# Issuing each 128-row gather as two gathers of 64 rows in a recurrent kernel's POOL stream

## The reference

```python
def step(h, inp):
    dAt, dBt, xt, Ct = inp
    h = dAt * h + dBt * xt[..., None]
    h_norm = jnp.sqrt(jnp.sum(h * h, axis=(1, 2), keepdims=True))
    scale = jnp.minimum(20.0 / (h_norm + 1e-08), 1.0)
    h = h * scale
    y = jnp.einsum('bdn,bn->bd', h, Ct) + Dp * xt
    return (h, y)
```

## Time and profile before

| | |
|---|---|
| device time, median of 3 runs | 1827.41 us (1826.48 to 1827.98) |
| the profiled execution's own time | 1828.65 us |
| its span, first to last instruction | 1826.9 us |
| busy: DVE | 1657.4 us, 91% |
| busy: PE | 1396.5 us, 76% |
| busy: ACT | 1082.4 us, 59% |
| busy: POOL | 932.5 us, 51% |
| L567, the power on POOL | 605.3 us in 1025 instructions |
| L539, gathers in the loop | 93.8 us in 80 instructions |
| L545, scatters | 91.9 us in 80 instructions |

### The profile page before, as it was taken

How to read it: one execution, slowest core, us unless ns; L and a number is a source line. 1 busy time by engine, 2 the same in 40 slices (tenths; PEclk the granted TensorE clock), 3 DMA queues, 4 the chain that set the end, 5 groups by cost and what they waited for, 6 DMA issues and landing times.

```text
span 1826.9 us, 38640 instructions
## 1 busy us (share of the span) xinstructions
PE 1396.5 (76%) x8889; PEld 1271.0 (70%) x8889; DVE 1657.4 (91%) x11513; ACT 1082.4 (59%) x2502; POOL 932.5 (51%) x1403
## 2 busy tenths in 40 slices
PE   6788979597968787697868786888859795879820
PEld 4577878496858687686758685877758685768720
DVE  7587999999998999999999999899999999899967
ACT  5775666556556654666565656566465655566424
POOL 5365555455555555455545554554555555555534
PEclk9858989898989899898989898898989898999965
DMA  9443011101020102100020102000110102010076
GB/s 334 149 202 95 20 32 45 51 19 35 19 76 23 30 19 65 31 23 29 21 74 24 30 24 71 22 25 27 41 51 22 35 19 74 21 31 22 18 247 223
DMA packets 97034, 110.47 MB, mean 60 GB/s; under 512 B 25680, under 2 KB 84176, under 8 KB 95632
## 3 DMA queue, kind: packets, MB, share of 16 engines
q1 hardware_dynamic: 87504, 86.26, 14.5%
q0 software_dynamic: 7776, 21.24, 3.7%
q10 hardware_dynamic: 1504, 0.22, 0.1%
HBM read 62.22 MB, written 45.48 MB: 59 GB/s over the span
## 4 chain that ended last, share of the span: by engine, by line
issue 38%; POOL 30%; DVE 22%; PE 6%; DMA 2%; POOLq 1%; ACT 1%; SPq 0%; DVEq 0%; ACTq 0%
POOL arena L567 22%; DVE arena L819 4%; DVE arena L790 3%; POOL moe L545 3%; POOL xrow L539 3%; DVE arena L804 3%; DVE arena L796 3%; DVE arena L811 3%; PE ps L1056 2%; DVE arena L815 1%; DVE arena L836 1%; DVE arena L793 1%; POOL arena L573 1%; DVE arena L808 1%; PE ps L1095 1%
## 5 line engine op out<-in xcount | busy, mean ns | idle before, releaser
L567 POOL TENSOR_TENSOR arena<-arena,neghalf 128x1 f32<-128x1 f32 x1025 | 605.3, 591 | 728.8 <-DVE arena L793 722.9
L815 DVE SCALAR_TENSOR_TENSOR arena<-arena 128x128 f32<-128x128 f32 x1024 | 360.5, 352 | 69.3 <-POOL arena L567 69.3
L1164 PE MATMUL ps<-ident,arena 128*128 128x128 f32 x1024 | 199.4, 319 | 228.8 <-ACT arena L908 190.1
L1164 PEld LDWEIGHTS ps<-ident,arena 128*128 128x128 f32 x1024 | 177.6, 245 | 252.7 <-issue 250.4
L983 ACT ACTIVATE arena<-ps,arena 128x128 f32<-128x128 f32 x1024 | 292.7, 373 | 53.7 <-PE ps L1168 52.8
L790 DVE TENSOR_TENSOR arena<-arena 128x128 f32<-128x128 f32 x1024 | 295.1, 288 | 23.6 <-issue 18.8
L1180 PE MATMUL ps<-arena,wf 128*128 128x256 f32 x1280 | 305.9, 387 | 10.9 <-ACT arena L995 10.9
L796 DVE CUSTOM_DVE_ANT_0 arena<-arena 128x128 f32<-128x128 f32 x1024 | 306.9, 300 | 0.0
L1168 PE MATMUL ps<-arena,pick 128*128 128x128 f32 x2048 | 286.6, 285 | 15.6 <-ACT arena L983 14.3
L804 DVE CUSTOM_DVE_ANT_0 arena<-arena 128x128 f32<-128x128 f32 x1024 | 292.6, 286 | 1.8 <-PE ps L1145 1.8
L1194 PE MATMUL ps<-wp,arena 128*128 128x256 f32 x1280 | 289.5, 379 | 0.0
(11 more groups left out here) (155 smaller groups left out, 1517.8 us busy)
## 6 DMA issues: line engine op xcount, KB each, us to landing
feed<-arena SPq DMA_DIRECT2D x9, 1024.0 KB, 3.9
arena<-feed SPq DMA_DIRECT2D x34, 256.0 KB
arena<-in_x SPq DMA_DIRECT2D x16, 512.0 KB, 6.4
moe<-zeros SPq DMA_DIRECT2D x8, 1024.0 KB, 9.5
wf<-in_c_fc SPq DMA_DIRECT2D x8, 1024.0 KB, 5.0
wp<-in_c_proj SPq DMA_DIRECT2D x8, 1024.0 KB, 6.0
arena<-moe SPq DMA_DIRECT2D x12, 512.0 KB, 8.6
arena<-dx SPq DMA_DIRECT2D x66, 64.0 KB
```

What stands on the lines that cost most here:

```text
L567: g.tensor_tensor(sv[:, slot, 1:2], mx, neghalf[:, 0:1], ALU.pow).then_inc(s_ready, 1)
L815: v.scalar_tensor_tensor(hr[:, slot, :], vv, sv[:, before, 1:2], ur[:, slot, :], ALU.mult, ALU.add)\
L1164: last = t.transpose(ps[q % 2][:, j * P:(j + 1) * P], tanhb[:, f, :, s], ident[:, :])
```

## The change

`gather` gets an argument `part`. Part 0 gathers 64 rows into partitions 0 to 63 of `xrow`, part 1 gathers 64 rows into partitions 64 to 127. Each of the 128-row gathers becomes one of each, so a turn has four gathers, in four consecutive steps: 2 to 5, 12 to 15, 36 to 39, 60 to 63, 84 to 87. The scatters stay as they are, in the same steps. The row numbers of part 1 lie in partitions 64 to 127 of slot_src; they are copied once, by one DMA from SP ahead of the loop, to `slot_hi` in partitions 0 to 63. In each round POOL copies ten columns of it to `hi_now`, beside the two copies that were there. The counts of `xrow_in` go from 32 to 64 a turn.

```diff
+        slot_hi = sb("slot_hi", [HALF, SC + EC], i32)
+        hi_now = sb("hi_now", [HALF, EC], i32)
...
-                    for c in range(2):
+                    for c in range(2 if kind == "down" else 4):
...
             sp.wait_ge(slots_ready, 1)
+            sp.dma_start(slot_hi[:, :], slot_src[HALF:P, :]).then_inc(hi_rows, 16)
             sp.wait_ge(stage_in, 32)
...
-            def gather(c, rows):
+            def gather(c, part, rows):
+                at = slice(part * HALF, (part + 1) * HALF)
-                g.indirect_dma_start(out=xrow[:, c, :], out_offset=None, in_=xnd,
+                g.indirect_dma_start(out=xrow[at, c, :], out_offset=None, in_=xnd,
...
-            gather(0, slot_src[:, 0:1])
-            gather(1, slot_src[:, 1:2])
+            pool.wait_ge(hi_rows, 16)
+            for c in range(2):
+                for part in range(2):
+                    gather(c, part, (slot_src[0:HALF], slot_hi)[part][:, c:c + 1])
...
-                        pool.wait_ge(xrow_in, m * (32 * TPE) + 32)
+                        pool.wait_ge(xrow_in, m * (64 * TPE) + 64)
...
+                        g.tensor_copy(hi_now[:, :], slot_hi[:, bass.ds(m * EC + 2, EC)]).then_inc(rows_staged, 1)
-                        pool.wait_ge(rows_staged, m * 2 + 2)
+                        pool.wait_ge(rows_staged, m * 3 + 3)
...
-                            gather(c, src_now[:, 2 * i + c:2 * i + c + 1])
+                            gather(c // 2, c % 2, (src_now[0:HALF], hi_now)[c % 2][:, 2 * i + c // 2:2 * i + c // 2 + 1])
...
-                                pe.wait_ge(xrow_in, m * (32 * TPE) + 32 * (i + 1))
+                                pe.wait_ge(xrow_in, m * (64 * TPE) + 64 * (i + 1))
```

More of the change, by code:

```diff
@@ L264, in build @@
         rows_staged = sem("rows_staged")
+        hi_rows = sem("hi_rows")
         loop_go = sem("loop_go")
```

## The result

| | before | changed |
|---|---|---|
| device time, median | 1827.20 us | 1859.65 us (1858.36 to 1860.40, 4 runs) |
| ratio | | 1.0177, 95% interval 1.0161 to 1.0193 |
| profiled span | 1826.9 us | 1858.3 us |
| forecast | | 1848 us (1801 to 1868), slower |

The kernel became 32.5 us slower; +20.6 had been forecast. The sign, the mechanism and the place were right; the size that was forecast is two thirds of what came.

The account below looks back on a forecast made before the run. POOL was taken as the bound in steps with a gather. Half gathers losing 59.2 us against 39.4 gave +19.8, the start +0.8: +20.6 us, so 1848 us from a median of 1827.41; range 1801 to 1868.

Parts of the forecast that it names:

- The bound and the room: Gather steps of the recurrence: POOL bounds them; 0.68 us per step is free, only a gather's excess is lost.
- G' = 1.05 us: Assumed time a 64-row gather holds POOL, mostly fixed cost; 59.2 us lost against 39.4, +19.8 us.
- the upper bound of 1.173: Half gather on POOL as long as a full one, if time doesn't depend on rows: +39.5 us.
- The hint from the power's fixed part: POOL's power instruction (L567): 419 of 591 ns fixed, 71%, hinting that a gather's cost is mostly fixed too.
- The third copy: POOL's hi_now copy in step 1: at most 0.19 us, fits 0.63 us idle, free; otherwise 1.5 us at most.
- The later landing: PE's transposes and ACT some 3.7 us later in experts 2 to 8; covered by 12.6 us lead, cost nothing.
- The rival's 26 us: Late gather landing reaches DVE through PE and ACT in experts 2 to 8: up to +26 us, 1874 us; chance 0.01.
- The start: Ahead of the loop: first gathers wait for slot_hi's DMA, ending about the first power; 0.8 us taken.

Follow-up runs that it names:

- the whole other part of the change: Kernel before plus only the slot_hi DMA, POOL's wait for it and the third copy, gathers kept at 128 rows: 1826.7 us, ratio 1.0001.
- the kernel with 64 rows: Kernel before, each gather fetching only the rows of partitions 0 to 63, same number of gathers, rows 64 to 127 left out: 1819.1 us, ratio 0.9962.
- the late scatter: Kernel before, each round's last scatter moved from step 120 to 127, its landing awaited in the next round's step 6: 1825.7 against 1827.8 us, ratio 0.9987.

## Why the prediction came out as it did

- **The bound and the room.** Right. DVE waits for POOL in each step with an indirect DMA and in no other, 240 times, as forecast. The room of 0.68 us gives 160 x (1.099 - 0.68) - 39.4 = +27.6 us for the gathers with the measured length; the steps show +26.7.
- **G' = 1.05 us.** Right in kind, mis-sized. A half gather takes 1.10 us, and this term of the sum is 160 x 0.05 = 8 us too small, the larger part of the miss. I had taken the middle of the two shortest full gathers. One was the second of two in a row without a power between (1.015), and such a one is shorter by itself: 0.96 for 64 rows where it is 1.10 behind a power (in the test with both halves in one step). The other (1.082) is the one behind the stall at 1258.29. Both were shorter because of their place, and in the changed kernel nearly all gathers stand right behind a power. The 1.10 us lie between my 1.05 and the upper bound of 1.173, a little nearer to mine; the length of a gather in its usual place, 1.146 us at the least, was in the trace.
- **The hint from the power's fixed part** (71%) pointed the right way; the gather's own is about 90%, 1.06 of 1.173 us. DMA: Bandwidth & Descriptors of the Trainium skill, section Anatomy of one DMA, calls the time of descriptor generation small and variable. By the rows that holds here: 0.9 ns a row, 0.12 of 1.173 us for 128. The overhead of emission, about 1 us in its section Latency and other measured facts, is near the 1.06 us.
- **The third copy.** Right: free, 0.44 us idle behind it, and 1.0001 for the whole other part of the change.
- **The later landing.** Right. PE waited 53.0 us, where about 49 were forecast. In expert 2 the copies of quad 5 ended at 380.22 + 1.14 = 381.36 and DVE's L812 of step 19 started at 391.94: 10.6 us of lead where there had been 12.6. The rival's 26 us didn't come.

```profile
372.85 1.11 PE L1135 MATMUL ps<-ident,xrow 128*128 128x128 f32 x4 [7.90 <-DMA xrow<-xnd,hi_now]
...
380.22 1.14 ACT L991 ACTIVATE arena<-ps,arena 128x128 f32<-128x128 f32 x4 [0.30 <-PE ps L1176]
...
391.94 0.28 DVE L812 CUSTOM_DVE_ANT_0 arena<-arena 128x128 f32<-128x128 f32 x1
```

- **The start.** The number was near, the path was not the one forecast: 0.8 us forecast, 1.2 us in the trace. slot_hi landed 1.8 us after its issue, where 5.0 were taken, and the four gathers were through at 151.37. POOL then stood idle for 2.16 us until DVE's L801 released the first power, so the gathers held nothing up. The first power comes anywhere from 152.03 to 153.80 us in the traces, and latest in the kernel with 64 rows, which has no second table; the near hit of this term is luck.

```profile
150.41 0.96 POOL L544 DMA_INDIRECT xrow<-xnd,slot_hi  x1 [0.30 <-issue]
153.53 0.62 POOL L574 TENSOR_TENSOR arena<-arena,neghalf 128x1 f32<-128x1 f32 x1 [2.16 <-DVE arena L801]
```

- **What wasn't there:** the DRAIN of POOL, +5.7 us, of which 4.65 are left in the time behind the last power. I had no term for the end of the program. Its row could have been read in the trace of before, as the last thing that POOL does, with 8.63 us; that it would grow by 5.7 could not.

## What to carry to other kernels

Before you split an instruction so that its pieces fit into idle time, measure the piece: an instruction that is nine tenths fixed costs nearly twice as much when halved. Find the room of one step (here 0.68 us), since only what exceeds it is lost, and move such an instruction to a step that has room already, instead of making it smaller (the late scatter brought some 2 us of 1827); and ask what in the last pass stands behind the wait that you moved along with it. Read the end of each engine's program too: work done there once can depend on how much was issued before.

## What the runs showed of the hardware

- An indirect DMA of 1 KB rows holds POOL for 1.173 us in the mean with 128 rows, 1.110 with 64 and 1.070 with 16, behind a power each time (a gather's group in the kernel before and in the two with fewer rows).
- Right behind another one it is shorter (0.96 us with 64 rows against 1.10), with a longer pause ahead of it (0.30 us against 0.17), in the kernel with both halves in one step.
- POOL stood still for 2.3 to 3.2 us ahead of the 114th indirect DMA (128 rows each) or the 129th (where some have fewer rows), and again ahead of the 224th with every block gathered twice. The recurrence lost about that time: the step with the stall took 4.07 us for 1.95 before, 4.76 for 1.87 in the changed kernel.
- POOL's DRAIN took from 5.9 to 14.7 us, and 0.08 us more for each indirect DMA added at the end. Why, and what makes it short again, is open.
